# Queries and keys of sequences 2 to 7 as three rounded matmuls, and small rows in PSUM

## The chip, the cores and the metric

One core of a Trainium2 chip runs the kernel. Its engines work side by side, each through its own queue in order: TensorE (PE, with its weight loads PEld), VectorE (DVE), ScalarE (ACT), GpSimd (POOL) and SyncE (SP), which issues most transfers. The metric is the device time of one execution in microseconds (us), the median over several runs. The kernel before takes 412.45 us (three runs, 410.89 to 412.59).

## The reference

Eight sequences of 512 tokens with 128 features go through two layers, all in fp32. Each layer is an attention-like part times the silu of a mixture of experts (MoE), added to the input. The change is in layer 1:

```python
xn = _layernorm(x)                       # layer 1, its own layernorm
q = elu(xn @ Wq.T + bq) + 1              # feature maps
k = elu(xn @ Wk.T + bk) + 1
v = xn @ Wv.T + bv
out = linear_attention(q, k, v)          # causal, chunks of 128, running key_sum, kv_sum
s = out @ Wo.T + bo
scores = softmax(xn @ gate_w.T); top 2 of 8 experts per token
g = silu( sum over the top 2 of scores * ((silu(xe @ w1) * (xe @ w3)) @ w2)
          + (silu(xn @ w1s) * (xn @ w3s)) @ w2s )
x = x + s * g
```

## The kernel before

The program has three stretches. Up to some 55 us it normalises the input, routes the tokens of layer 0, and scatters them by group. Up to some 179 us it runs layer 0's experts on 35 sorted tiles, with layer 0's recurrences beside them. The rest is layer 1, one sequence `j` after the other, 0 to 7. The change lies in this last stretch.

Layer 1 is written out by hand as slots: every engine's queue runs `for j in range(8): for u in range(18)`, and its `if u == ...` lines say which piece stands in which slot. All experts are computed for all tokens: 8 experts and one shared unit, each with a gate half and an up half, give 18 slots.

- **PE** starts each slot with `gate_up(j, u)` (lines 948 to 966). To compute an fp32 product faster than fp32 matmuls do, the product is made of three fp32r ("rounded") matmuls into one PSUM bank: weights rounded times input rounded (L964), weights rounded times the input's rest (L965), weights' rest times input rounded (L966), where rest is value minus rounded value. In odd slots a `unit_down` (fp32, L986) follows. The attention pieces lie between: `scores` (L916) in slots 0 and 2, `sum_state` (L931), `turn_scores` (L910) in slot 5, `turn_result` (L991) in 7, `attend` (L943, L945) in 8.
- Sequence `k+1 = j+2` is prepared in the later slots of `j`: `turn_xn1` (four transposes, L891) in slot 13, `values` (L898) in 14, `query` (L903) in 15 and `key` (L906) in 16. `query` and `key` are plain fp32 matmuls of `a1w` with `xn1T`; the profile counts two matmuls for each.
- **DVE** empties each gate or up half with `scaled` (L1478: PSUM times the spread scores, to `gu`). `gate_up` of a slot waits until `scaled` of three slots earlier is done (`m_free`, a ring of three banks). Beside it: `variances` (L1356 to L1359) in slot 7, `ranks` and `scored` (L1388 to L1393) in 1 and 3, `gated` (L1343) and `added` (L1346) in 4 and 5.
- **ACT** applies silu (`unit_silu`, L658, table functions), copies `xn1T` out of PSUM (`xn1T_out`, L614) in slot 14 and rounds it (`round_of`, L619) in slot 5 of the next sequence, where it stands before `state_out` and `scoreT_out`.
- **POOL** multiplies the halves (`hidden1`, L443), makes `xc_rest` (`rest_of`, L430), the scales (L423, L425), `qT` and `kT` (`query_or_key`, L437), the result (L448) and the gathers of layer 0's output (L409).

The rounded input and its rest, `xc_round` and `xc_rest`, are kept in two buffer pairs, used in turn by even and odd sequences. `e1`, `pr` and `mv1` (the router's exponentials, its probabilities, the layernorm's means and variances) lie in SBUF: 128 partitions by 32, 32 and 8 values. A semaphore wait stands ahead of each instruction that needs another engine's result; `link` makes DVE wait for its own last result.

Of the kernel before, what the change touches and what calls it, by code (L numbers as in the profile page):

```python
# [6 lines left out]
ALU = mybir.AluOpType  # L7
# [47 lines left out]
REC_BANKS = (SEQS - LATE) * (6,) + LATE * (5,)  # L55
BANKS = (0, 1, 7)
CHUNK = TPS // 2
SCORE_BANKS = (6, 6, 4, 4)
# [25 lines left out]
def gated_recurrent_moe_two_layers(  # L84
# [4 lines left out]
    with ctx:  # L89
        def sb(name, shape, dt=F32):  # L90
            return ctx.enter_context(nc.sbuf_tensor(name, shape, dt))
# [24 lines left out]
        w0d = sb("w0d", [P, GROUPS * D0])  # L116
        a1w = sb("a1w", [P, 3 * P])
        a1b = sb("a1b", [P, 3])
        a1bn = sb("a1bn", [P, 2])
# [94 lines left out]
        def in_one_place(earlier, last):  # L214
# [25 lines left out]
        h0, h0T, gu = in_one_place(  # L240
            [[("h0", [P, 2, 512], F32), ("h0T", [P, 2, 512], F32)]], [("gu", [P, RING, 2, SEQ], F32)])

        HALF_E = E1 // 2 * SEQ
# [7 lines left out]
            w0_rounded w0_split f_turned f_xT f_xr f_gate f_up f_sg f_h f_hT f_hTs f_down f_y  # L251
            c_gy c_var c_rstd c_xn c_turned c_xT c_round c_rest w13_split c_q c_k c_relu c_expq c_qkT
            c_v c_lg c_lgm c_exp c_scores c_scoreT c_scoreT_out c_a c_at c_keys c_keys_out c_state c_state_out c_num c_s1
# [120 lines left out]
        def _(pool):  # L374
# [38 lines left out]
            def split_w13(p):  # L413
# [4 lines left out]
                                   ALU.subtract).then_inc(s["w13_split"], 1)  # L418

            def scales(k):  # L420
                pool.wait_ge(s["c_var"], k + 1)
                wait(pool, "c_xn", k)
                pool.tensor_tensor(rstd1[:, :], var1[:, :], minus_half[:, 0:TPS], ALU.pow).then_inc(s["c_rstd"], 1)  # L423
                pool.wait_ge(s["c_rstd"], 2 * k + 1)
                pool.tensor_tensor(nmr1[:, :], nmr1[:, :], rstd1[:, :], ALU.mult).then_inc(s["c_rstd"], 1)  # L425

            def rest_of(k):
                pool.wait_ge(s["c_round"], k + 1)
                wait(pool, "m_gu", SLOTS * (k - 1))
                pool.tensor_tensor(xc_rest[k % 2][:, :], xn1T[:, :], xc_round[k % 2][:, :].bitcast(F32),  # L430
                                   ALU.subtract).then_inc(s["c_rest"], 1)
# [22 lines left out]
            for p in range(PAIRS + 1):  # L454
                split_w13(p)
            gather(0)
            gather(1)
# [6 lines left out]
            for j in range(SEQS):  # L464
                hidden1(j, 1)
                if 0 < j < SEQS - 1:
                    query_or_key(j + 1, 1)
                hidden1(j, 2)
                if j + 1 < SEQS:
                    rest_of(j + 1)  # L470
                hidden1(j, 3)
                if j + 2 < SEQS:
                    scales(j + 2)
                if j == 0:
                    query_or_key(1, 1)
                hidden1(j, 4)
                if 0 < j < SEQS - 1:
                    query_or_key(j + 1, 0)
                if j > 0:
                    result1(j - 1)  # L480
                hidden1(j, 5)
                if j < PSEQ[1]:
                    gather(PSEQ[0] + j, slice(0, 2))
                if j == 0:
                    query_or_key(1, 0)
                hidden1(j, 6)
                if j < PSEQ[1]:
                    gather(PSEQ[0] + j, slice(2, 4))
                hidden1(j, 7)
                hidden1(j, 8)  # L490

        @block.scalar
        def _(act):
# [206 lines left out]
            for j in range(SEQS):  # L700
                k = j + 1
                for u in range(SLOTS):
                    if u == (0 if j < LAST else 1):
                        unit_silu(j, 0)
                    if u == 11 and k + 1 < SEQS:
                        normalised(k + 1)
# [8 lines left out]
                    if j == 0:  # L715
# [7 lines left out]
                        if u == 12:  # L723
                            scoreT_out(1, 4)
                    if u == 1 and 0 < j < SEQS - 1:
                        softmax_exp(k)
                        feature_exp(k)
                    if u == (1 if j == 0 else 5) and k < SEQS:
                        round_of(k)
                    if u == 1 and j == 0:  # L730
# [3 lines left out]
                    if k + 1 < SEQS:  # L734
                        if u == 3:
                            gy_silu(k + 1)
                        if u == 14:
                            xn1T_out(k + 1, 6)
                        if u == 16:
# [9 lines left out]
        def _(pe):  # L749
# [144 lines left out]
            def values(k, pair, bank):  # L894
# [4 lines left out]
                last.then_inc(s["c_v"], 1)  # L899

            def query(k, bank):
                pe.wait_ge(s["c_xT"], k + 1)
                pe.matmul(ps[:, bank, :], a1w[:, 0:P], xn1T[:, :], start=True, stop=True).then_inc(s["c_q"], 1)  # L903
# [45 lines left out]
            def gate_up(j, u):  # L949
                e, part = divmod(u, 2)  # L950
                n = SLOTS * j + u
                if u == 0:
                    pe.wait_ge(s["c_rest"], j + 1)
# [4 lines left out]
                par = j % 2  # L958
                last = n == SLOTS * SEQS - 1
# [90 lines left out]
            for j in range(SEQS):  # L1050
                k = j + 1
                for u in range(SLOTS):
# [62 lines left out]
        def _(dve):  # L1115
# [237 lines left out]
            def variances(k):  # L1353
                wait(dve, "c_xn", k)
                for t in range(TPS):
                    last = nc.vector.bn_aggr(mv1[:, t, :], st1[:, t, :])  # L1356
                link(last)
                nc.vector.tensor_scalar(nmr1[:, :], mv1[:, :, 0], -1.0, None, ALU.mult)
                nc.vector.tensor_scalar(var1[:, :], mv1[:, :, 1], LN_EPS, None, ALU.add).then_inc(s["c_var"], 1)  # L1359

            def values_out(k, pair, bank):
# [24 lines left out]
            def scored(k):  # L1386
                dve.wait_ge(s["c_exp"], k + 1)
                link(nc.vector.tensor_reduce(rs[:, :], e1[:, :, :], AX_X, ALU.add))  # L1388
# [4 lines left out]
                nc.vector.scalar_tensor_tensor(score[:, :, :].rearrange("p e t -> p t e"), rank[:, :, :], float(TOPK1),  # L1393
                                               pr[:, :, :], ALU.is_lt, ALU.mult).then_inc(s["c_scores"], 1)

# [92 lines left out]
            for j in range(SEQS):  # L1488
                k = j + 1
                for u in range(SLOTS):  # L1490
# [30 lines left out]
                    if k + 1 < SEQS:  # L1521
# [78 lines left out]
```

## Time and profile before

| | us |
|---|---|
| median of three runs | 412.45 |
| the profiled execution | 407.45 |
| its span, first to last instruction | 405.1 |
| PE busy in the span | 380.5 (94%) |
| DVE busy | 267.9 (66%) |
| ACT busy | 225.2 (56%) |
| POOL busy | 219.7 (54%) |
| mean granted TensorE clock | 0.975 of full |

Matmuls are pipelined: a record of 592 ns for half an fp32 product contains the time in which the next is already streaming. In the chain of work that ended last, where one piece begins when the one before lets go, the same product has 0.86 us for both halves. The sections below take the cost of PE work from the chain, and the cost on the other engines from the means of single instructions.

### The profile page before, as it was taken

The numbers are of one execution on the slowest core, as the hardware profiler recorded it, in microseconds if no ns is written. First come the engines' busy times: TensorE is split into PE (matmuls) and PEld (weight loads), VectorE is DVE, ScalarE is ACT, GpSimd is POOL, SyncE is SP. The second block draws the span as 40 slices with busy tenths as digits, with TensorE's granted clock in tenths as the row PEclk, the third lists the DMA queues.
The fourth block names the chain that finished last, engine by engine and source line by source line (L and its number), as shares of the span: only waits on it lengthen the run. The fifth ranks groups of instructions, "written<-read, shape, count | busy, mean of one in ns | idle before, by whom it ended". The sixth has DMA issues, their size and how long they took to land.

```text
span 405.1 us, 6272 instructions
## 1 busy us (share of the span) xinstructions
PE 380.5 (94%) x1874; PEld 285.3 (70%) x1874; DVE 267.9 (66%) x745; ACT 225.2 (56%) x447; POOL 219.7 (54%) x211
## 2 busy tenths in 40 slices
PE   7999877699997999899999999999999999999996
PEld 5684346588886888787667667677677677676784
DVE  5979943463342356528879769679689498677563
ACT  3685973355543565869664483574474664742321
POOL 4437887252007015106775857867949849267451
PEclk9868999899999899999999999999999999999999
DMA  8995311510031001036050150330510701503300
GB/s 229 270 359 230 107 39 52 151 38 2 0 104 47 9 2 28 0 124 209 24 214 0 43 220 0 117 145 2 212 51 0 262 1 29 207 0 98 139 26 26
DMA packets 26590, 38.63 MB, mean 95 GB/s; under 512 B 2496, under 2 KB 22848, under 8 KB 24128
## 3 DMA queue, kind: packets, MB, share of 16 engines
q1 hardware_dynamic: 24512, 34.03, 25.3%
q0 software_dynamic: 2048, 4.23, 3.4%
q8 instruction: 16, 0.26, 0.3%
q14 instruction: 14, 0.11, 0.1%
HBM read 29.20 MB, written 9.05 MB: 94 GB/s over the span
## 4 chain that ended last, share of the span: by engine, by line
PE 65%; DVE 11%; ACT 11%; issue 6%; another core or an unknown queue 4%; DMA 1%; POOL 1%; SPq 0%; DVEq 0%; ACTq 0%
PE ps L986 9%; PE ps L861 6%; PE ps L966 6%; PE ps L964 6%; PE ps L965 6%; PE ps L841 3%; PE ps L871 3%; PE ps L782 3%; PE ps L843 3%; PE ps L842 3%; PE ps L945 3%; PE ps L898 2%; PE ps L981 2%; DVE score L1393 2%
## 5 line engine op out<-in xcount | busy, mean ns | idle before, releaser
L443 POOL TENSOR_TENSOR gu<-gu 128x512 f32<-128x512 f32 x64 | 84.3, 1322 | 58.4 <-DVE gu L1478 53.5
L964 PE MATMUL ps<-xc_round,w_round 128*128 128x512 f32 (+1 forms) x145 | 82.2, 567 | 0.6 <-DVE gu L1456 0.6
L658 ACT ACTIVATE gu<-gu 128x512 f32<-128x512 f32 x64 | 40.4, 630 | 74.8 <-DVE gu L1478 74.7
L986 PE MATMUL ps<-gu,w2s 128*128 128x512 f32 x126 | 64.3, 592 | 0.0
L966 PE MATMUL ps<-xc_round,w_rest 128*128 128x512 f32 (+1 forms) x145 | 57.0, 393 | 0.0
L965 PE MATMUL ps<-xc_rest,w_round 128*128 128x512 f32 (+1 forms) x145 | 56.8, 392 | 0.0
L1478 DVE TENSOR_TENSOR gu<-ps,w_raw 128x512 f32<-128x512 f32 x64 | 43.7, 687 | 17.8 <-PE ps L966 14.9
L1319 DVE TENSOR_TENSOR sx_rest<-ps,sx_round 128x128 fp32r<-128x128 f32 x35 | 10.2, 292 | 64.4 <-ACT sx_round L571 58.5
L409 POOL DMA_INDIRECT xnT<-sorted_y,slot x32 | 31.3, 977 | 36.2 <-DMA sorted_y<-sorted_sb 28.4
L580 ACT COPY h0T<-ps 128x512 f32<-128x512 f32 x35 | 20.5, 587 | 52.2 <-PE ps L871 37.2
L861 PEld LDWEIGHTS ps<-w0d,h0T 128*128 128x128 f32 x280 | 37.7, 197 | 12.3 <-issue 9.5
L861 PE MATMUL ps<-w0d,h0T 128*128 x280 | 38.7, 283 | 8.2 <-ACT sorted_sb L585 7.2
L399 POOL DMA_INDIRECT sorted_rows<-sorted_sb,slot x32 | 37.2, 1161 | 14.8 <-issue 9.5
L841 PE MATMUL ps<-w_round,sx_round 128*128 x70 | 34.4, 492 | 5.2 <-DVE sx_rest L1319 3.8
L964 PEld LDWEIGHTS ps<-xc_round,w_round 128*128 128x128 f32 x145 | 27.5, 190 | 15.1 <-issue 11.4
L965 PEld LDWEIGHTS ps<-xc_rest,w_round 128*128 128x128 f32 x145 | 27.5, 190 | 13.7 <-issue 12.0
L1329 DVE SCALAR_TENSOR_TENSOR h<-sg,sorted_sb,ps 128x256 f32<-128x256 f32 x70 | 30.2, 473 | 4.0 <-PE ps L871 2.6
L966 PEld LDWEIGHTS ps<-xc_round,w_rest 128*128 128x128 f32 x145 | 27.2, 188 | 6.1
L1478 DVE TENSOR_TENSOR gu<-ps,w0d 128x512 f32<-128x512 f32 x32 | 21.7, 688 | 14.0 <-PE ps L966 13.9
L843 PE MATMUL ps<-w_rest,sx_round 128*128 x70 | 27.9, 399 | 0.0
L842 PE MATMUL ps<-w_round,sx_rest 128*128 x70 | 27.8, 398 | 0.0
L986 PEld LDWEIGHTS ps<-gu,w2s 128*128 128x128 f32 x126 | 23.6, 188 | 5.5 <-POOL gu L443 0.2
(203 smaller groups left out, 778.7 us busy)
## 6 DMA issues: line engine op xcount, KB each, us to landing
w_raw<-score_rows SPq DMA_DIRECT2D x8, 1024.0 KB
sorted_sb<-score_rows SPq DMA_DIRECT2D x4, 1024.0 KB
w0d<-score_rows SPq DMA_DIRECT2D x4, 1024.0 KB
sorted_rows<-zero_rows SPq DMA_DIRECT2D x1, 2340.0 KB, 15.6
xa<-in_x SPq DMA_DIRECT2D x8, 256.0 KB, 4.9
w_raw<-in_gate_up SPq DMA_DIRECT2D x1, 2048.0 KB
out_x<-xa SPq DMA_DIRECT2D x7, 256.0 KB
sorted_sb<-sorted_rows SPq DMA_DIRECT2D x1, 1690.0 KB, 7.9
```

The costliest lines, as they stand in the source:

```text
L399: pool.indirect_dma_start(sorted_rows, bass.IndirectOffsetOnAxis(ap=slot[:, t:t + 1], axis=0), rows[:, t, :], None).then_inc(scattered[h], 16)
L443: pool.tensor_tensor(gu[:, e % RING, 1, :], gu[:, e % RING, 0, :], gu[:, e % RING, 1, :], ALU.mult).then_inc(s["m_h"], 1)
L658: nc.scalar.activation(gu[:, e % RING, 0, :], gu[:, e % RING, 0, :], ACT.Silu).then_inc(s["m_sg"], 1)
L841: pe.matmul(bank, sx_round[:, par, :], w0_round[:, c], start=True, stop=False)
L842: pe.matmul(bank, sx_rest[:, par, :], w0_round[:, c], start=False, stop=False)
L843: return pe.matmul(bank, sx_round[:, par, :], w0_rest[:, c], start=False, stop=True)
L861: last = pe.matmul(ps[:, bank, 0:P], h0T[:, par, c * P:(c + 1) * P], w0d[:, bass.ds(g + c * P, P)], start=(c == 0), stop=(c == HC - 1))
L964: pe.matmul(bank, w13_round[:, c], xc_round[par][:, some], start=True, stop=False)
L965: pe.matmul(bank, w13_round[:, c], xc_rest[par][:, some], start=False, stop=False)
L966: pe.matmul(bank, w13_rest[:, c], xc_round[par][:, some], start=False, stop=True).then_inc(s["m_gu"], 1)
L986: pe.matmul(ps[:, 3, :], w2s[:, w * P:(w + 1) * P], gu[:, e % RING, 1, :], start=(e == 0), stop=(e == E1)).then_inc(s["m_y"], 1)
L1478: nc.vector.tensor_tensor(gu[:, p % RING, part, :], ps[:, BANKS[u % RING], :], spread[j % 2][(e - 1) // (E1 // 2)][:, c:c + SEQ], ALU.mult ...
```

## The change

For sequences 2 to 7 the query and key products are made of three fp32r matmuls (`in_three`), like the experts' products. POOL rounds the two weight matrices once and takes their rest (`split_qk`), after the same work for the experts' weights. Rounded input and rest must now be there before the queries, so they are made earlier: ACT rounds right behind `xn1T_out`, both now in slot 13, and DVE instead of POOL makes the rest, in slot 14, out of the PSUM bank that the transposes wrote. As the former sequences' buffers are still being read then, there is a third buffer pair, `xc2_round` and `xc2_rest`, in the place of an array that layer 0's weights used. PE's `turn_xn1` moves from slot 13 to slot 12, and ACT's `normalised` from slot 11 to 10 (which leaves its place in the queue as it was, since no silu stands between).

For the same sequences `e1`, `pr` and `mv1` lie in PSUM bank 6. ACT's softmax exponential writes there, so it now waits for DVE's first two masks of that bank (`c_at`), and stands behind the exponential of queries and keys instead of ahead of it.

```diff
+SMALL_BANK = 6
+        qk_round = sb("qk_round", [P, 2 * P], F32R)
+        qk_rest = sb("qk_rest", [P, 2 * P], F32R)
-        at, w0_round = in_one_place(
-            [[("at", [P, TPS, SEQ], F32)]], [("w0_round", [P, GROUPS * 2 * GU0], F32R)])
+        at, xc2_round, xc2_rest, w0_round = in_one_place(
+            [[("at", [P, TPS, SEQ], F32), ("xc2_round", [P, SEQ], F32R), ("xc2_rest", [P, SEQ], F32R)]],
+            [("w0_round", [P, GROUPS * 2 * GU0], F32R)])
-        xc_round, xc_rest = (xc0_round, xc1_round), (xc0_rest, xc1_rest)
+        xc_round, xc_rest = (xc0_round, xc1_round, xc2_round), (xc0_rest, xc1_rest, xc2_rest)
+        def small(first, n):
+            return ps[:, SMALL_BANK, first:first + n].rearrange("p (t c) -> p t c", t=TPS)
+        def e1_of(k):
+            return e1[:, :, :] if k < 2 else small(0, TPS * E1)
+        # pr_of(k), mv1_of(k): likewise
...
 POOL
+            def split_qk():
+                pool.wait_ge(s["attn1_in"], 16 * 4)
+                pool.tensor_copy(qk_round[:, :], a1w[:, 0:2 * P]).then_inc(s["qk_split"], 1)
+                pool.wait_ge(s["qk_split"], 1)
+                pool.tensor_tensor(qk_rest[:, :], a1w[:, 0:2 * P], qk_round[:, :].bitcast(F32),
+                                   ALU.subtract).then_inc(s["qk_split"], 1)
-                if j + 1 < SEQS:
-                    rest_of(j + 1)
+                if j == 0:
+                    rest_of(1)
...
 ACT
             def xn1T_out(k, bank):
-                wait(act, "c_rest", k)
+                if k in (1, 2):
+                    act.wait_ge(s["c_rest"], k)
             def round_of(k):
-                wait(act, "m_gu", SLOTS * (k - 1))
-                nc.scalar.copy(xc_round[k % 2][:, :], xn1T[:, :]).then_inc(s["c_round"], 1)
+                wait(act, "m_gu", SLOTS * (k - 2))
+                nc.scalar.copy(xc_round[k % 3][:, :], xn1T[:, :]).then_inc(s["c_round"], 1)
             def softmax_exp(k):
+                if k > 1:
+                    act.wait_ge(s["c_at"], TPS * (k - 1) + CHUNK)
-                nc.scalar.activation(e1[:, :, :], lg[:, :, :], ACT.Exp).then_inc(s["c_exp"], 1)
+                nc.scalar.activation(e1_of(k), lg[:, :, :], ACT.Exp).then_inc(s["c_exp"], 1)
...
 PE
+            def in_three(k, i, bank):
+                rest_ready(k)                    # waits c_rest_dve
+                pe.wait_ge(s["qk_split"], 2)
+                c, par = slice(i * P, (i + 1) * P), k % 3
+                pe.matmul(ps[:, bank, :], qk_round[:, c], xc_round[par][:, :], start=True, stop=False)
+                pe.matmul(ps[:, bank, :], qk_round[:, c], xc_rest[par][:, :], start=False, stop=False)
+                return pe.matmul(ps[:, bank, :], qk_rest[:, c], xc_round[par][:, :], start=False, stop=True)
-                        if u == 13:
+                        if u == 12:
                             turn_xn1(k + 1, 6)
-                            query(k + 1, 6)
+                            in_three(k + 1, 0, 6).then_inc(s["c_q"], 1)
-                            key(k + 1, 5)
+                            in_three(k + 1, 1, 5).then_inc(s["c_k"], 1)
...
 DVE
+            def rest_of(k, bank):
+                dve.wait_ge(s["c_round"], k + 1)
+                nc.vector.tensor_tensor(xc_rest[k % 3][:, :], ps[:, bank, :], xc_round[k % 3][:, :].bitcast(F32),
+                                        ALU.subtract).then_inc(s["c_rest_dve"], 1)
-                    last = nc.vector.bn_aggr(mv1[:, t, :], st1[:, t, :])
+                    last = nc.vector.bn_aggr(both[:, t, :], st1[:, t, :])     # both = mv1_of(k)
-                link(nc.vector.tensor_tensor(pr[:, :, :], e1[:, :, :], rs[:, :].unsqueeze(2).broadcast_to([P, TPS, E1]),
+                link(nc.vector.tensor_tensor(pr_of(k), e1_of(k), rs[:, :].unsqueeze(2).broadcast_to([P, TPS, E1]),
+                        if u == 14:
+                            rest_of(k + 1, 6)
```

How the queues stand in slots 12 to 16 of a middle sequence. PE before, from the last of `values` in slot 14 (L898) to the key in slot 16 (L906), with the query (L903) between:

```order
L898 MATMUL ps<-vg_w,xn1T 128x136 [waits c_xT,c_s1]
L898 MATMUL ps<-vg_w,xn1T 128x136
L964 MATMUL ps<-xc_round,w_round 128x512 [waits m_free]
L965 MATMUL ps<-xc_rest,w_round 128x512
L966 MATMUL ps<-xc_round,w_rest 128x512
L986 MATMUL ps<-gu,w2s 128x512 [waits m_h]
L903 MATMUL ps<-xn1T,a1w 128x512 [waits c_xT]
L964 MATMUL ps<-xc_round,w_round 128x512 [waits m_free]
L965 MATMUL ps<-xc_rest,w_round 128x512
L966 MATMUL ps<-xc_round,w_rest 128x512
L906 MATMUL ps<-xn1T,a1w 128x512
```

PE now, from slot 15's down product (L1027) on: L1005 to L1007 are the experts' three, L938 to L940 the new three.

```order
L1027 MATMUL ps<-gu,w2s 128x512 [waits m_h]
L938 MATMUL ps<-xc_round,qk_round 128x512 [waits qk_split,c_rest_dve]
L939 MATMUL ps<-xc_rest,qk_round 128x512
L940 MATMUL ps<-xc_round,qk_rest 128x512
L1005 MATMUL ps<-xc_round,w_round 128x512 [waits m_free]
L1006 MATMUL ps<-xc_rest,w_round 128x512
L1007 MATMUL ps<-xc_round,w_rest 128x512
L938 MATMUL ps<-xc_round,qk_round 128x512 [waits qk_split,c_rest_dve]
L939 MATMUL ps<-xc_rest,qk_round 128x512
L940 MATMUL ps<-xc_round,qk_rest 128x512
```

The query waits for DVE's rest where it waited for ACT's copy. DVE before, the `scaled` of slots 13 to 15 (L1478) and the first `values_out` (L1366, L1368):

```order
L1478 TENSOR_TENSOR gu<-ps,w_raw 128x512 [waits m_y,m_gu]
L1478 TENSOR_TENSOR gu<-ps,w_raw 128x512 [waits m_h,m_gu]
L1478 TENSOR_TENSOR gu<-ps,w_raw 128x512 [waits m_y,m_gu]
L1366 TENSOR_TENSOR vo<-ps,bv_wo 128x2x128 [waits c_exp,c_num,c_v]
L1368 COPY lg<-ps 128x16
```

DVE now, the same slots (L1525 is `scaled`, L1414 the new rest, L1408 and L1410 `values_out`):

```order
L1525 TENSOR_TENSOR gu<-ps,w_raw 128x512 [waits m_y,m_gu]
L1525 TENSOR_TENSOR gu<-ps,w_raw 128x512 [waits m_h,m_gu]
L1414 TENSOR_TENSOR xc_rest<-ps,xc_round 128x512 [waits c_round]
L1525 TENSOR_TENSOR gu<-ps,w_raw 128x512 [waits m_y,m_gu]
L1408 TENSOR_TENSOR vo<-ps,bv_wo 128x2x128 [waits c_exp,c_num,c_v]
L1410 COPY lg<-ps 128x16
```

The rest stands between two `scaled`, ahead of the one of slot 15. ACT before, and then now, from the silus of slots 11 and 13 (L658, now L684) on:

```order
L658 ACTIVATE gu<-gu 128x512 [waits m_free] x2
L614 COPY xn1T<-ps 128x512 [waits c_rest,c_k,c_turned]
L658 ACTIVATE gu<-gu 128x512 [waits m_free]
L624 ACTIVATE tv<-ps,a1b 128x512 [waits c_qkT,c_q]
L625 ACTIVATE tg<-ps,a1bn 128x512
```

```order
L684 ACTIVATE gu<-gu 128x512 [waits m_free] x2
L638 COPY xn1T<-ps 128x512 [waits c_k,c_turned]
L643 CAST xc_round<-xn1T 128x512 [waits m_gu,c_xT]
L684 ACTIVATE gu<-gu 128x512 [waits m_free]
L648 ACTIVATE tv<-ps,a1b 128x512 [waits c_qkT,c_q]
```

The copy keeps its place behind the silu of slot 13; the rounding is new behind it, and is gone from the next sequence's slot 5.

## Rows read from the trace of the kernel before

**Rows 1.** Windows: us, then each engine's busy time (instructions), PE clock, DMA share, GB/s.

```profile
235.20:263.50 28.30, 28.07 (x125) 19.70 (x124) 22.68 (x55) 16.08 (x29) 20.67 (x19) 1.00 0.26 95
```

**Rows 2.** Chain of waits, sequence 2: start us, us, what.

```profile
237.40 0.65 PE ps L916 x4
...
245.60 0.28 PE ps L910
245.88 0.23 PE ps L964
...
258.22 0.07 issue
258.29 1.16 PE ps L898 x8
...
261.00 0.86 PE ps L903 x2
261.86 0.23 PE ps L964
...
262.56 0.86 PE ps L906 x2
```

**Rows 3.** Chain of waits, sequences 0 and 7.

```profile
198.21 0.11 PE ps L910
...
375.01 0.65 PE ps L916 x4
...
383.04 0.23 PE ps L964
```

**Rows 4.** Timeline of sequence 2, DVE and POOL: start us, us, engine, line, operation.

```profile
242.73 0.17 DVE L1388 TENSOR_REDUCE rs<-e 128x4 f32<-128x32 f32 x1
242.96 1.29 POOL L443 TENSOR_TENSOR gu<-gu 128x512 f32<-128x512 f32 x1 [3.76 <-DVE gu L1478]
243.15 1.15 DVE L1390 TENSOR_TENSOR pr<-e,rs 128x32 f32<-128x32 f32 x1
244.21 1.26 POOL L437 TENSOR_TENSOR kT<-tv,tg 128x512 f32<-128x512 f32 x1
244.33 1.21 DVE L1393 SCALAR_TENSOR_TENSOR score<-rank,pr 128x32 f32<-128x32 f32 x1
...
246.04 0.68 DVE L1343 TENSOR_TENSOR gy<-gy,sT 128x512 f32<-128x512 f32 x1
...
250.42 1.28 POOL L443 TENSOR_TENSOR gu<-gu 128x512 f32<-128x512 f32 x1
250.59 1.13 DVE L1358 TENSOR_SCALAR nmr<-mv 128x4 f32<-128x4 f32 x1
```

**Rows 5.** Single lines of DVE: count, shortest/median/longest ns, first and last start.

```profile
L1390 DVE TENSOR_TENSOR pr<-e,rs x8: 193/1144/1154, 169.7 to 355.9; 128x32 f32<-128x32 f32 x8
L1393 DVE SCALAR_TENSOR_TENSOR score<-rank,pr x8: 215/1212/1218, 169.9 to 357.1; 128x32 f32<-128x32 f32 x8
L1358 DVE TENSOR_SCALAR nmr<-mv x8: 170/1126/1133, 145.5 to 335.2; 128x4 f32<-128x4 f32 x8
L1478 DVE TENSOR_TENSOR gu<-ps,w_raw x64: 675/691/693, 196.5 to 384.5; 128x512 f32<-128x512 f32 x64
```

**Rows 6.** Timeline of sequence 2, slots 12 to 14, DVE and ACT.

```profile
256.20 1.28 DVE L1478 TENSOR_TENSOR gu<-ps,w_raw 128x512 f32<-128x512 f32 x2
256.92 0.63 ACT L658 ACTIVATE gu<-gu 128x512 f32<-128x512 f32 x1 [1.50 <-DVE gu L1478]
257.56 0.59 ACT L614 COPY xn1T<-ps 128x512 f32<-128x512 f32 x1
258.26 0.69 DVE L1478 TENSOR_TENSOR gu<-ps,w_raw 128x512 f32<-128x512 f32 x1 [0.78 <-PE ps L966]
```

**Rows 7.** Groups by line: busy us, mean ns of one, idle before and releaser.

```profile
L430 POOL TENSOR_TENSOR xc_rest<-xn1T,xc_round 128x512 fp32r<-128x512 f32 x8 | 10.2, 1272 | 5.9 <-ACT xc_round L619 5.9
L634 ACT ACTIVATE tg<-tg 128x1024 f32<-128x1024 f32 x8 | 8.4, 1045 | 0.0
```

More of the change, by code:

```diff
@@ L241, in gated_recurrent_moe_two_layers, with pr_of, mv1_of @@
             [[("h0", [P, 2, 512], F32), ("h0T", [P, 2, 512], F32)]], [("gu", [P, RING, 2, SEQ], F32)])
+        def small(first, n):
+            return ps[:, SMALL_BANK, first:first + n].rearrange("p (t c) -> p t c", t=TPS)
+        def e1_of(k):
+            return e1[:, :, :] if k < 2 else small(0, TPS * E1)
+        def pr_of(k):
+            return pr[:, :, :] if k < 2 else small(TPS * E1, TPS * E1)
+        def mv1_of(k):
+            return mv1[:, :, :] if k < 2 else small(2 * TPS * E1, 2 * TPS)
         HALF_E = E1 // 2 * SEQ
@@ L251, in gated_recurrent_moe_two_layers @@
             w0_rounded w0_split f_turned f_xT f_xr f_gate f_up f_sg f_h f_hT f_hTs f_down f_y
-            c_gy c_var c_rstd c_xn c_turned c_xT c_round c_rest w13_split c_q c_k c_relu c_expq c_qkT
+            c_gy c_var c_rstd c_xn c_turned c_xT c_round c_rest c_rest_dve w13_split qk_split c_q c_k c_relu c_expq c_qkT
             c_v c_lg c_lgm c_exp c_scores c_scoreT c_scoreT_out c_a c_at c_keys c_keys_out c_state c_state_out c_num c_s1
@@ L428, in rest_of @@
                 pool.wait_ge(s["c_round"], k + 1)
-                wait(pool, "m_gu", SLOTS * (k - 1))
-                pool.tensor_tensor(xc_rest[k % 2][:, :], xn1T[:, :], xc_round[k % 2][:, :].bitcast(F32),
+                pool.tensor_tensor(xc_rest[k % 3][:, :], xn1T[:, :], xc_round[k % 3][:, :].bitcast(F32),
                                    ALU.subtract).then_inc(s["c_rest"], 1)
@@ L455, in _ @@
                 split_w13(p)
+            split_qk()
             gather(0)
@@ L704, in _ @@
                         unit_silu(j, 0)
-                    if u == 11 and k + 1 < SEQS:
+                    if u == 10 and k + 1 < SEQS:
                         normalised(k + 1)
@@ L725, in _ @@
                     if u == 1 and 0 < j < SEQS - 1:
+                        feature_exp(k)
                         softmax_exp(k)
-                        feature_exp(k)
-                    if u == (1 if j == 0 else 5) and k < SEQS:
-                        round_of(k)
+                    if u == 1 and j == 0:
+                        round_of(1)
                     if u == 1 and j == 0:
@@ L736, in _ @@
                             gy_silu(k + 1)
-                        if u == 14:
+                        if u == 13:
                             xn1T_out(k + 1, 6)
+                            round_of(k + 1)
                         if u == 16:
@@ L899, in values, with rest_ready @@
                 last.then_inc(s["c_v"], 1)
+            def rest_ready(k):
+                if k < 2:
+                    pe.wait_ge(s["c_rest"], k + 1)
+                else:
+                    pe.wait_ge(s["c_rest_dve"], k - 1)
+            def in_three(k, i, bank):
[5 more added lines that the diff above has]
+                return pe.matmul(ps[:, bank, :], qk_rest[:, c], xc_round[par][:, :], start=False, stop=True)
             def query(k, bank):
@@ L952, in gate_up @@
                 if u == 0:
-                    pe.wait_ge(s["c_rest"], j + 1)
+                    rest_ready(j)
                 e = unit_at(j, e)
@@ L957, in gate_up @@
                 wait(pe, "m_free", n - RING + 1)
-                par = j % 2
+                par = j % 3
                 last = n == SLOTS * SEQS - 1
@@ L1354, in variances @@
                 wait(dve, "c_xn", k)
+                both = mv1_of(k)
                 for t in range(TPS):
-                    last = nc.vector.bn_aggr(mv1[:, t, :], st1[:, t, :])
+                    last = nc.vector.bn_aggr(both[:, t, :], st1[:, t, :])
                 link(last)
-                nc.vector.tensor_scalar(nmr1[:, :], mv1[:, :, 0], -1.0, None, ALU.mult)
-                nc.vector.tensor_scalar(var1[:, :], mv1[:, :, 1], LN_EPS, None, ALU.add).then_inc(s["c_var"], 1)
+                nc.vector.tensor_scalar(nmr1[:, :], both[:, :, 0], -1.0, None, ALU.mult)
+                nc.vector.tensor_scalar(var1[:, :], both[:, :, 1], LN_EPS, None, ALU.add).then_inc(s["c_var"], 1)
             def values_out(k, pair, bank):
@@ L1387, in scored @@
                 dve.wait_ge(s["c_exp"], k + 1)
-                link(nc.vector.tensor_reduce(rs[:, :], e1[:, :, :], AX_X, ALU.add))
+                link(nc.vector.tensor_reduce(rs[:, :], e1_of(k), AX_X, ALU.add))
                 link(nc.vector.reciprocal(rs[:, :], rs[:, :]))
-                link(nc.vector.tensor_tensor(pr[:, :, :], e1[:, :, :], rs[:, :].unsqueeze(2).broadcast_to([P, TPS, E1]),
+                link(nc.vector.tensor_tensor(pr_of(k), e1_of(k), rs[:, :].unsqueeze(2).broadcast_to([P, TPS, E1]),
                                              ALU.mult))
@@ L1393, in scored @@
                 nc.vector.scalar_tensor_tensor(score[:, :, :].rearrange("p e t -> p t e"), rank[:, :, :], float(TOPK1),
-                                               pr[:, :, :], ALU.is_lt, ALU.mult).then_inc(s["c_scores"], 1)
+                                               pr_of(k), ALU.is_lt, ALU.mult).then_inc(s["c_scores"], 1)
             dve.wait_ge(sorted_in[0], 16)
```

## The prediction

> **What bounds the kernel now.** I read three views in this order: the windows by sequence, to see which engine is full in layer 1; the chain of waits through one sequence, to see where that engine is late; then the timeline around each such place, to see why. In the window of sequence 2, TensorE is busy for 28.07 of 28.30 us at a granted clock of 1.00, DVE for 22.68, POOL for 20.67, ACT for 16.08 [rows 1]. So layer 1 is bound by PE, and the reader should expect that work on another engine pays only where PE waits for it.
>
> The chain shows two such waits in each sequence. The first is at `turn_scores` (L910), which starts at 245.60, right behind DVE's score [rows 2, 4]. Its size comes from two equal stretches, from the first `scores` to the start of slot 6's product. In sequence 2 it is 245.88 - 237.40 = 8.48 us. In sequence 7 the same PE work is done without L910: 383.04 - 375.01 = 8.03 us. L910 takes 0.11 us where nobody is waited for [rows 3]. That leaves 8.48 - 8.03 - 0.11 = 0.34 us of waiting. As it is one sequence of six, read to a few hundredths, I take 0.3. The second wait is 0.07 us ahead of `values` (L898), for the copy `xn1T` [rows 2]: the copy ends at 257.56 + 0.59 = 258.15 and L898 starts at 258.29 [rows 2, 6].
>
> Why is the score late? The multiply for `pr`, 32 values per partition, takes 1.15 us, and the score 1.21 us. The shortest of the same lines are 0.19 and 0.22 us [rows 4, 5]. Each long one ends within 0.1 us of the end of a POOL instruction that had begun before it: 244.30 against 244.25, 245.54 against 245.47. The `nmr` of the variances does so too, 251.72 against 251.70 [rows 4]. All three have only SBUF operands. `scaled` (L1478), one operand in PSUM and one in SBUF, varies by 18 ns over 64 instructions, though POOL is busy most of the time [rows 1, 5]. So DVE stands still behind POOL in these three, and does not in instructions with an operand in PSUM.
>
> The Trainium skill ("SBUF — State Buffer", section "Who interferes with whom") has this as a rule: a DVE instruction with two SBUF inputs, or a 2-port mode one such as tensor_scalar, shares a port pair with GpSimd, and the second to start blocks wholly. The trace agrees for the three. The rule also speaks against the change: `gated` (L1343) has two SBUF inputs, and the change brings it forward into POOL's time. That is weighed below.
>
> **The change part by part.**
> *Queries and keys.* An fp32 product takes 0.86 us of the chain, 261.86 - 261.00. An expert's three take 262.56 - 261.86 = 0.70 us [rows 2]. The new three have the same shapes. Each replaced product gives back 0.16 us; with two for each of sequences 2 to 7, 12 x 0.16 = 1.9 us. That lies on the path, as PE is full. The three measured here begin right behind an fp32 product, which is where the query's will begin too (behind the down product of slot 15), so I take no extra.
>
> *Small rows in PSUM.* Of the three blocked instructions `pr` and the score lose up to 1.15 - 0.19 = 0.96 and 1.21 - 0.22 = 0.99 us, so the score comes 1.95 us earlier, against 0.3 us that PE waits. The wait goes in each of sequences 1 to 6: 6 x 0.3 = 1.8 us. Behind it L910 waits for nothing else. The exponential that feeds the score moves behind ACT's longer one, 1.04 us later [rows 7]. That one begins in slot 1, and DVE's first read of the result at 242.73 [rows 4] is in slot 3, two product slots and a down product later on PE (over 2 us), so I count 0 and would see a late exponential as an idle DVE ahead of its first sum. No row before shows DVE writing to PSUM. Bounds for `pr`: 0.19 us as if unblocked, 1.15 us as if still blocked. At either end the score alone, which has one SBUF input left, gives 0.99 us, three times the wait. `nmr` saves 0.95 us of DVE, off the path.
>
> *Turn one slot earlier.* The transposes cost PE the same in slot 12. Their data is ready without help: the transposes before came after a down product (0.86) and a gate product (0.70) more, and ACT's normalising stands at the same place in its queue. The copy to `values` now has 0.70 + 0.86 us more of cover, but stands behind the silu of slot 13, which starts only after `scaled` of slot 12. That silu runs 256.92 to 257.55 and the copy ends 258.15 [rows 6], so if DVE were as late as now, the 0.07 us would stay. DVE is less late by nearly the 0.95 us of `nmr`, so I count the 0.07 as gone: 6 x 0.07 = 0.4 us; its lower bound is 0.
>
> *Rounding and rest.* ACT's rounding, as wide as its copy (0.59 us), only changes place, and follows the copy by 0.6: done near 258.8 at the latest. DVE's rest is as wide as `scaled` and has its operand kinds, 0.69 us [rows 5]. It follows `scaled` of slot 14, which ends 258.26 + 0.69 = 258.95 [rows 6], so the rest is there at 259.6. The query stands at 261.00 [rows 2]: cover 1.4 us. Both sides move together when PE gains. Behind the rest on DVE wait `scaled` of slot 15 and `values_out`; slot 15's product ends on PE after 260.1, so they are not held. DVE's sum over a sequence: -0.96 - 0.99 - 0.95 + 0.69 = -2.2 us. POOL loses 1.27 us [rows 7], which stood ahead of its product for slot 7 and the scales; nothing on PE waits for these now, so I count 0.
>
> *Rounding the weights on POOL*, once, two instructions, is cheaper than one rest and rounding of the experts' 512 columns. It lies before the gathers, where POOL waits for layer 0's output; 0.
>
> Sum: 1.9 + 1.8 + 0.4 = 4.1 us. The profiled execution took 407.45 us (span 405.1), so it would take 403.3. The median of before is 5.0 us above that execution; nothing in layer 1's clock (1.00) explains it, and I take the difference to stay: 412.45 - 4.1 = 408.4 us, 1.0% faster.
>
> **The rivals.**
> *A. The rows in PSUM free nothing*, since the destination in PSUM or the remaining SBUF operand still keeps DVE behind POOL. Then PE goes on waiting 0.3 us, and only 1.9 to 2.3 us come: about 410.3. For it: no row shows such a write. Against it: the 18 ns of L1478 [rows 5].
>
> *B. Part of it is given back.* `gated` now follows a score that ends near 243.6, and `scaled` after it near 244.4, inside POOL's L437, which runs 244.21 to 245.47; before it stood at 246.04, free, 0.68 us [rows 4]. Blocked, it costs DVE up to 1.1 us, as `pr` and the score do now. `scaled` of slot 5 then ends near 246.8, and the PE product that needs its bank is slot 8's, near 248.1 after the gain (L910 at 245.3, then products of 0.70, 0.70, 0.86 and the turned result, by the chain's prices). So it is covered by more than 1 us. By the skill's rule the wait would merely move from two instructions that PE awaits to one that it doesn't; by the sum it costs 0. If two such blocks fall together, PE loses 0.2 to 0.5 us a sequence: 409.5 to 411.5.
>
> *C. Slower: the new preparation is late.* One mechanism: ACT's copy stands behind the silu of slot 13, that behind DVE's `scaled` of slot 12. Now they start at 256.20, 256.92 and 257.56, one right behind the other [rows 6], and the copy is just in time for PE. If a blocked time such as that of `pr` and the score together, 0.96 + 0.99 = 1.95 us, fell ahead of that `scaled`, the copy would come as much later, and PE would stand 1.9 us before `values`, six times: 408.4 + 11.4 = 419.8 us. It decides from 4.1 / 6 = 0.7 us of PE wait per sequence. Against it: DVE has 2.2 us less to do, and the block on `nmr`, which makes it late there, goes.
>
> **How the numbers follow.** Forecast 0.64, A 0.10, B 0.17, C 0.05; 0.04 for a gain above 6 us, if DVE's and POOL's lead also shortens stretches in sequences 0 and 7. The likeliest gives 408.4 us. The low end has half of those 4 us more: 406.4. The high end takes in A and most of B: 411.3. What a measurement tells from no change is about 0.5%, 2.1 us: faster means under 410.4. The forecast is nearly wholly there, A half, B a third: 0.78. Slower is C and a little: 0.06. The same: 0.16.
>
> **What would show it.** Right: one L910 without DVE ahead of it and 0.11 us in the chain; `pr` and the score near 0.2 us, `nmr` near 0.17 us; three 0.23 us pieces for query and key; 0.7 us less for each sequence than before; no DVE piece in the chain of sequences 1 to 6. Wrong: an idle PE ahead of `values` or of the first new part, which names ACT or DVE (C); `pr` still at 1.15 us (A); `gated` at 1.7 us with PE waiting for a bank in slot 8 (B). A clock below 1.00 in layer 1 would upset all of it.

## The result, and the profile after

| | before | after |
|---|---|---|
| median of four runs, us | 411.67 | 403.59 |
| lowest and highest | 408.44, 412.59 | 402.41, 403.96 |
| the profiled execution | 407.45 | 403.38 |
| its span | 405.1 | 400.5 |

The ratio is 0.9899, with a 95% interval of 0.9850 to 0.9948. All later runs were on three chips on which the kernel before took 400.4 to 400.6 us. There the changed kernel took 395.28 us against 400.63: 0.9860 (0.9823 to 0.9896). The kernel is faster, by 1.0 to 1.4%. One execution of a later kernel (`pr` in SBUF) took 626.42 us at a mean granted clock of 0.557; its ratio below leaves it out.

As the whole time differs between the first comparison and the later ones by more than the change is worth, all that follows is read from layer 1, where the granted clock is 1.00 (but for two stretches of the last experiment). The measure is the period of a sequence: the time from the first `attend` piece of one to that of the next in the chain of waits. Of the chain before (start us, us, what), the first and the last of six that bound the middle sequences:

```profile
221.01 0.67 PE ps L945 x6
...
362.00 0.67 PE ps L945 x6
```

After, the same two:

```profile
221.06 0.67 PE ps L986 x6
...
357.46 0.67 PE ps L986 x6
```

Five periods took 362.00 - 221.01 = 140.99 us, 28.20 each, and now 136.40 us, 27.28 each: 0.92 us less. Over six sequences that is 5.5 us. The span is only 4.6 us shorter, since layer 1 started about 1 us later in this execution. The microsecond was lost in layer 0: in both traces PE stood still for some 3.5 us until 132.5 us, and from 132 to 138 us the granted clock was then 0.50, where before it was 0.72; from 138 to 182 us it was 1.00 in both. The traces of the later runs have no such stand there, and their layer 1 starts some 8 us sooner (the first `attend` of the changed kernel at 187.30 us, here at 195.68). The periods don't depend on it: the later trace of the changed kernel has 27.29 us.

The window that answers to [rows 1], after:

```profile
235.20:263.50 28.30, 28.30 (x130) 20.66 (x129) 23.25 (x57) 17.24 (x31) 21.02 (x19) 1.00 0.32 115
```

PE is busy for all of it. The chain of waits of the same sequence, to be laid beside [rows 2]:

```profile
244.40 0.45 PE ps L972 x4
244.85 0.11 PE ps L951
...
257.07 0.24 PE ps L1007
257.30 0.93 PE ps L925 x8
...
258.92 0.86 PE ps L1027 x2
259.78 0.23 PE ps L938
260.01 0.24 PE ps L939
260.25 0.23 PE ps L940
```

No DVE, ACT or issue piece is left. `turn_scores` (L951) takes its bare 0.11 us. The query is three pieces of 0.23 to 0.24 us (L938 to L940). And `values` (L925) takes 0.93 us, where L898 took 1.16 behind a wait of 0.07 [rows 2]: the prediction had no step for that.

The single lines of DVE that answer to [rows 5] (count, shortest/median/longest ns, first and last start), and POOL's `kT`:

```profile
L1437 DVE TENSOR_TENSOR ps<-ps,rs x6: 198/200/200, 215.2 to 351.6; 128x32 f32<-128x32 f32 x6
L1440 DVE SCALAR_TENSOR_TENSOR score<-rank,ps x6: 208/211/215, 215.5 to 351.8; 128x32 f32<-128x32 f32 x6
L1400 DVE TENSOR_SCALAR nmr<-ps x6: 160/161/163, 194.9 to 330.3; 128x4 f32<-128x4 f32 x6
L1384 DVE TENSOR_TENSOR gy<-gy,sT x8: 680/682/702, 142.8 to 325.3; 128x512 f32<-128x512 f32 x8
L1387 DVE SCALAR_TENSOR_TENSOR xa<-gy,xa x8: 691/1050/1061, 143.5 to 326.7; 128x512 f32<-128x512 f32 x8
L459 POOL TENSOR_TENSOR kT<-tv,tg x8: 1272/1750/1767, 186.4 to 352.7; 128x512 f32<-128x512 f32 x8
```

`pr`, the score and `nmr` now take 0.20, 0.21 and 0.16 us in all six sequences. That POOL is busy beside them shows in the timeline of sequence 2, to be laid beside [rows 4]:

```profile
242.30 1.29 POOL L465 TENSOR_TENSOR gu<-gu 128x512 f32<-128x512 f32 x1 [3.32 <-DVE gu L1525]
...
242.51 0.20 DVE L1437 TENSOR_TENSOR ps<-ps,rs 128x32 f32<-128x32 f32 x1
...
242.74 0.21 DVE L1440 SCALAR_TENSOR_TENSOR score<-rank,ps 128x32 f32<-128x32 f32 x1
...
243.50 0.68 DVE L1384 TENSOR_TENSOR gy<-gy,sT 128x512 f32<-128x512 f32 x1
243.56 1.77 POOL L459 TENSOR_TENSOR kT<-tv,tg 128x512 f32<-128x512 f32 x1
...
244.83 1.05 DVE L1387 SCALAR_TENSOR_TENSOR xa<-gy,xa 128x512 f32<-128x512 f32 x1
```

`gated` (L1384) isn't blocked; POOL's `kT`, which starts inside it, is (1.75 us at the median, where the one of [rows 4] took 1.26), and so is `added` (L1387) behind it. Nobody on PE waits for either.

The preparation, in DVE's and ACT's timeline of the same sequence:

```profile
255.41 0.63 ACT L684 ACTIVATE gu<-gu 128x512 f32<-128x512 f32 x1 [1.60 <-DVE gu L1525]
255.95 0.57 ACT L638 COPY xn1T<-ps 128x512 f32<-128x512 f32 x1
256.55 0.62 ACT L643 CAST xc_round<-xn1T 128x512 fp32r<-128x512 f32 x1
257.95 0.68 DVE L1414 TENSOR_TENSOR xc_rest<-ps,xc_round 128x512 fp32r<-128x512 f32 x1
```

The copy ends at 256.52, 0.8 us ahead of `values`; the rest ends at 258.63, 1.15 us ahead of the query. The first weight load of `values`, shown next, begins at 256.91: from the copy to that it is 0.4 us.

Why is `values` shorter? PEld's timeline shows it. Here `xn1T` is the stationary operand, so the first weight load itself needs the copy. Before:

```profile
258.26 0.99 PEld L898 LDWEIGHTS ps<-vg_w,xn1T 128*128 128x128 f32 x8 [0.48 <-issue]
258.29 0.47 PE L898 MATMUL ps<-vg_w,xn1T 128*128 128x136 f32 x2
```

After:

```profile
256.91 1.12 PEld L925 LDWEIGHTS ps<-vg_w,xn1T 128*128 128x128 f32 x8
257.14 1.09 PE L925 MATMUL ps<-vg_w,xn1T 128*128 128x136 f32 x8
```

Now the first load is done while the gate product still streams, and the matmul follows 0.23 us behind the start of the load. Before, load and matmul began together, after the wait, and the load was paid for by PE. The same shows at `turn_scores`, whose stationary operand is the score. Before, its load began only when DVE's score was done, 0.01 us ahead of the transpose at 245.60 [rows 2]:

```profile
245.59 0.09 PEld L910 LDWEIGHTS ps<-cst,score 128*32 128x32 f32 x1 [0.36 <-DVE score L1393]
```

The piece took 0.28 us there and takes 0.11 now. Of the 0.3 us priced as a wait, 0.17 were this.

### The profile page after: what moved, and what is told of

The parts are those of the page before. It is cut to its first block, busy times and chain, and to the rows that moved or that the text cites. A ratio compares the mean times of both kernels' runs of the same rounds, so it can differ in the third digit from the quotient of the medians.

```text
span 400.5 us, 6309 instructions
## 1 busy us (share of the span) xinstructions
PE 375.9 (94%) x1886; PEld 289.1 (72%) x1886; DVE 262.2 (65%) x751; ACT 226.5 (57%) x447; POOL 215.3 (54%) x207
## 4 chain that ended last, share of the span: by engine, by line
PE 77%; ACT 11%; issue 4%; another core or an unknown queue 3%; DVE 2%; DMA 1%; SPq 1%; POOL 1%; ACTq 0%; DVEq 0%
PE ps L1027 13%; PE ps L1007 8%; PE ps L1005 8%; PE ps L1006 8%; PE ps L888 7%; PE ps L868 4%; PE ps L869 3%; PE ps L898 3%; PE ps L870 3%; PE ps L986 3%; PE ps L957 2%; PE ps L809 2%; PE ps L1022 2%; PE ps L925 2%
## 5 line engine op out<-in xcount | busy, mean ns | idle before, releaser
L465 POOL TENSOR_TENSOR gu<-gu 128x512 f32<-128x512 f32 x64 | 85.2, 1334 | 58.1 <-DVE gu L1525 54.6
L1005 PE MATMUL ps<-xc_round,w_round 128*128 128x512 f32 (+1 forms) x145 | 79.7, 549 | 0.6 <-DVE gu L1503 0.5
L684 ACT ACTIVATE gu<-gu 128x512 f32<-128x512 f32 x64 | 40.4, 631 | 65.2 <-DVE gu L1525 60.6
L1027 PE MATMUL ps<-gu,w2s 128*128 128x512 f32 x126 | 64.3, 592 | 0.0
L1007 PE MATMUL ps<-xc_round,w_rest 128*128 128x512 f32 (+1 forms) x145 | 57.1, 394 | 0.0
L1525 DVE TENSOR_TENSOR gu<-ps,w_raw 128x512 f32<-128x512 f32 x64 | 43.9, 688 | 19.6 <-PE ps L1007 16.8
L415 POOL DMA_INDIRECT sorted_rows<-sorted_sb,slot x32 | 36.1, 1129 | 14.8 <-issue 9.5
L868 PE MATMUL ps<-w_round,sx_round 128*128 x70 | 35.3, 504 | 3.8 <-DVE sx_rest L1360 3.8
L1005 PEld LDWEIGHTS ps<-xc_round,w_round 128*128 128x128 f32 x145 | 27.4, 189 | 14.0 <-issue 8.8
L1007 PEld LDWEIGHTS ps<-xc_round,w_rest 128*128 128x128 f32 x145 | 27.2, 187 | 6.0
L1525 DVE TENSOR_TENSOR gu<-ps,w0d 128x512 f32<-128x512 f32 x32 | 22.0, 687 | 14.0 <-PE ps L1007 14.0
L1027 PEld LDWEIGHTS ps<-gu,w2s 128*128 128x128 f32 x126 | 23.7, 188 | 5.4
```

Of the source, the lines that this page charges most:

```text
L415: pool.indirect_dma_start(sorted_rows, bass.IndirectOffsetOnAxis(ap=slot[:, t:t + 1], axis=0), rows[:, t, :], None).then_inc(scattered[h], 16)
L465: pool.tensor_tensor(gu[:, e % RING, 1, :], gu[:, e % RING, 0, :], gu[:, e % RING, 1, :], ALU.mult).then_inc(s["m_h"], 1)
L684: nc.scalar.activation(gu[:, e % RING, 0, :], gu[:, e % RING, 0, :], ACT.Silu).then_inc(s["m_sg"], 1)
L868: pe.matmul(bank, sx_round[:, par, :], w0_round[:, c], start=True, stop=False)
L1005: pe.matmul(bank, w13_round[:, c], xc_round[par][:, some], start=True, stop=False)
L1007: pe.matmul(bank, w13_rest[:, c], xc_round[par][:, some], start=False, stop=True).then_inc(s["m_gu"], 1)
```

## The experiments

One chip ran the changed kernel, the rows alone, both with fp32 queries, and the changed one with rows in SBUF; a second the turn in slot 13, `pr` and `mv1` in SBUF and the copy in slot 15; a third the other two. Kernels of one chip share the runs of the kernel before, whose period is read from its one trace, that of the first comparison. "Period" is the mean of the five; "`values`" is its piece in the chain. Ratios are to the kernel before, with the 95% interval.

| kernel | period us | `values` us | ratio |
|---|---|---|---|
| before | 28.20 | 1.16 + 0.07 wait | |
| turn in slot 12 alone | 28.13 | 1.09 | 0.9970 (0.9943 to 0.9997) |
| rows in PSUM alone | 27.93 | 1.17 + 0.07 wait | 0.9946 (0.9919 to 0.9973) |
| both, fp32 queries and keys | 27.64 | 0.93 | 0.9895 (0.9863 to 0.9927) |
| changed, rows in SBUF | 27.79 | 1.09 to 1.10, once 1.17 behind a wait | 0.9916 (0.9881 to 0.9950) |
| changed, turn in slot 13 | 27.58 | 1.17 + 0.07 wait | 0.9910 (0.9871 to 0.9948) |
| changed | 27.28 | 0.93 | 0.9860 (0.9823 to 0.9896) |
| changed, `pr` in SBUF | 27.28 | 0.93 | 0.9835 (0.9746 to 0.9925) |
| changed, `mv1` in SBUF | 27.28 | 0.93 | 0.9841 (0.9773 to 0.9909) |
| changed, only `e1` in PSUM | 27.29 | 0.93, once 1.00 | 0.9860 (0.9817 to 0.9903) |
| changed, copy in slot 15 | 30.17 | 1.17 + 2.0 wait, twice more at a lower clock | 1.0265 (1.0192 to 1.0338) |

**The changed kernel again**, beside its parts.

> The changed kernel once more, to have it in the same rounds as its parts. Its trace has 27.28 us per sequence against 28.2 before; six such gains are 5.5 us, 1.3 to 1.4% of the time. If the rest of the program is the same, the ratio is 0.986 to 0.987; the first run's 0.990 is then its low side.

The period is that of the first comparison to a hundredth of a microsecond. This ratio, unlike the first, leaves the forecast's 0.990 just outside its interval, on the side of a larger gain.

**Rows in PSUM alone.** The kernel before, with

```diff
+        def e1_of(k):
+            return e1[:, :, :] if k < 2 else small(0, TPS * E1)     # pr_of, mv1_of likewise
+                if k > 1:
+                    act.wait_ge(s["c_at"], TPS * (k - 1) + CHUNK)
-                        softmax_exp(k)
                         feature_exp(k)
+                        softmax_exp(k)
```

> Only the small rows go to PSUM (with the wait and the order of the exponentials that this needs); queries and keys stay fp32, the turn stays in slot 13. My theory: L910 no longer waits, 0.3 us per sequence, while the wait ahead of values stays, since the copy hangs on the turn in slot 13: 27.9 us per sequence, 1.8 us in all, ratio 0.995 to 0.996. Rival: DVE's lead of some 2.9 us also frees the values, then 27.6 us per sequence and 3.6 us in all.

The period fell by 0.27 us: this is the wait at `turn_scores`. But `values` still waited, though `nmr` was short. The chain, and ACT's copy in the timeline:

```profile
251.19 0.07 issue
251.26 1.17 PE ps L912 x8
```

```profile
250.53 0.59 ACT L626 COPY xn1T<-ps 128x512 f32<-128x512 f32 x1 [0.58 <-PE ps L905]
```

ACT stood idle for 0.58 us ahead of the copy, until the transposes (L905) were done. So it is PE's own transposes that make the copy late in slot 13, even when ACT is free. In the kernel before, the silu ends at 257.55 [rows 6] and the transposes, by the chain, at 257.52: two releasers within 0.03 us, of which I had named one.

**The turn alone.** The kernel before, with

```diff
-                        if u == 13:
+                        if u == 12:
                             turn_xn1(k + 1, 6)
```

> The kernel before with nothing but the turn in slot 12. In the run with three-part products and rows in SBUF, the copy hung on the silu of slot 13 and values took 1.10 us without a wait ahead. My theory: the same here, as DVE is as late as before: the 0.07 us go and values lose 0.07 of their 1.17, so 28.2 - 0.14 = 28.05 us per sequence, the wait at L910 stays. Rival: the turn alone frees the values, 0.93 us, 27.9 us per sequence.

The wait ahead of `values` goes, but only just: with DVE as late as before, the copy stands behind the silu again. Chain, and PEld:

```profile
249.28 0.23 PE ps L966
249.51 1.09 PE ps L898 x8
```

```profile
249.40 0.76 PEld L898 LDWEIGHTS ps<-vg_w,xn1T 128*128 128x128 f32 x6 [0.33 <-issue]
```

The copy ends at 249.29, the first load begins at 249.40, too late to hide, and `values` takes 1.09 us. PE didn't stand still ahead of it here, and still it cost 0.16 us more than 0.93; so it isn't the stand as such that makes `values` dear, as one of the expectations below has it, but the late load. The kernel lost 1.23 - 1.09 = 0.14 us there, yet four of its periods are 28.11 to 28.12 us, 0.08 less than before's, and the fifth is 28.20. Where the rest went back is open.

**Both, with fp32 queries and keys.** The kernel of the rows alone, with the turn in slot 12.

> Rows in PSUM and the turn in slot 12, queries and keys in fp32 with two buffer pairs. My theory: both waits go, values take 0.93 us instead of 1.16, as an engine that has stood still needs some 0.2 us more for its next group: 28.2 - 0.3 - 0.3 = 27.6 us per sequence; the changed kernel's 27.28 is then 0.32 less, 2 x 0.16. Rival: the 0.23 us of values have nothing to do with the wait but with the three-part neighbours; then values stay at 1.16 us and the sequence at 27.8.

```profile
248.82 0.23 PE ps L980
249.05 0.93 PE ps L912 x8
```

0.93 us needs both edits: the turn frees the copy from the transposes, the rows free it from a late silu. Against the rows alone the turn is worth 0.30 us a sequence (27.93 to 27.64, before rounding 27.932 to 27.636), where alone it was worth 0.07. And from here to the changed kernel is 27.64 - 27.28 = 0.36 us, the price of two products: 0.18 each. In the chain the two new products take 0.70 and 0.69 us in place of 0.86 each; the last 0.03 us of the 0.36 lie in hundredths of their neighbours.

**The changed kernel with the rows in SBUF.**

```diff
         def e1_of(k):
-            return e1[:, :, :] if k < 2 else small(0, TPS * E1)
+            return e1[:, :, :]                                      # pr_of, mv1_of likewise
```

> The changed kernel with the small rows left in SBUF: the three-part queries and keys, the third buffer pair, the turn in slot 12. My theory: the 0.3 us at L910 stays, the products give 12 x 0.16 = 1.9 us; the values' wait depends on whether DVE is late at the scaled of slot 12. If it goes: 28.2 - 0.32 - 0.3 = 27.6 us per sequence; if it stays: 27.9. Rival: without the rows in PSUM DVE gets the rest on top of its blocked time and PE waits ahead of the first new part, over 28.2 us per sequence, slower than before.

The blocks are back, with `turn_scores` at 0.28 us behind them, and `values` starts just in time, at 1.10 us:

```profile
L1437 DVE TENSOR_TENSOR pr<-e,rs x8: 193/1143/1149, 161.2 to 344.7; 128x32 f32<-128x32 f32 x8
L1440 DVE SCALAR_TENSOR_TENSOR score<-rank,pr x8: 215/1212/1216, 161.5 to 345.9; 128x32 f32<-128x32 f32 x8
```

```profile
248.34 0.24 PE ps L1007
248.58 1.10 PE ps L925 x8
```

Four of its periods are 27.71 to 27.74 us; one is 28.04, with a real wait ahead of `values`. Without the rows the preparation stands at the edge.

**The changed kernel with the turn in slot 13.**

```diff
-                        if u == 12:
+                        if u == 13:
                             turn_xn1(k + 1, 6)
```

> The changed kernel with the turn back in slot 13; ACT's copy and rounding and DVE's rest stay where they are. My theory: the copy then hangs on the turn, PE waits 0.07 us ahead of values and these take 1.17 us: 27.28 + 0.30 = 27.6 us per sequence, +1.8 us in all. The rest still comes over 1 us ahead of the query. Rival: the rest comes too late as well, PE waits ahead of the first new part, and the sequence takes over 28 us.

0.30 us a sequence came back, 0.07 as a wait and 0.24 in `values`. The rest was still there for the query: the earlier turn isn't needed for the three parts.

**`pr`, then `mv1`, back in SBUF; then both.** Three kernels, each the changed one with

```diff
         def pr_of(k):                                               # or mv1_of, or both
-            return pr[:, :, :] if k < 2 else small(TPS * E1, TPS * E1)
+            return pr[:, :, :]
```

> The changed kernel with pr in SBUF, e1 and mv1 in PSUM. pr then has one SBUF input, the score two. My theory: pr takes 0.2 us, the score is blocked by POOL for about 1 us, and since it alone is late PE does not wait at L910: 27.28 us per sequence. Rival: what blocks is the SBUF destination; then pr takes over 1 us too, and L910 waits as before, 27.6 us.

> The changed kernel with mv1 in SBUF, e1 and pr in PSUM. My theory: nmr is blocked again or not, by where POOL stands; even at 1.1 us DVE has caught up by slot 12, since pr and the score no longer delay it: 27.28 us per sequence, values 0.93. Rival: it was nmr's place right ahead of slots 8 to 12 that made the copy late; then values wait again, 27.5 to 27.6 us.

> The changed kernel with only e1 in PSUM, pr and mv1 in SBUF. With pr alone in SBUF the score took 0.94 us, with mv1 alone nmr took 1.11 us, each at no cost to PE. My theory: both together still cost PE nothing, 27.28 us per sequence, since the score at 0.94 us ends ahead of L910 and DVE has caught up by slot 12: e1 alone carries the gain of the rows. Rival: the two blocks add up as in the kernel before, the copy comes late and values take 1.1 us or more: 27.45 to 27.6 us.

The single lines with `pr` in SBUF:

```profile
L1437 DVE TENSOR_TENSOR pr<-ps,rs x6: 191/191/192, 207.3 to 343.7; 128x32 f32<-128x32 f32 x6
L1440 DVE SCALAR_TENSOR_TENSOR score<-rank,pr x8: 219/938/942, 163.0 to 343.9; 128x32 f32<-128x32 f32 x8
L1384 DVE TENSOR_TENSOR gy<-gy,sT x8: 684/1208/1216, 134.9 to 318.1; 128x512 f32<-128x512 f32 x8
```

The multiply reads `e1` from PSUM and isn't blocked, wherever it writes; in sequence 2 it starts 0.20 us behind the start of a POOL product of 1.29 us. The score, now with both inputs in SBUF, is (0.94 us), and so is `gated`, which meets a POOL instruction in the new place (1.21 us). `nmr` with `mv1` in SBUF is blocked again (1.11 us at the median). No mean period moved by more than 0.01 us: one of the two blocks, of 0.96 and 0.99 us, was enough to take away, and `mv1` is off the path. `e1` alone in PSUM gives nearly all of it. But two of its six `values` took more, the first 1.11 us (ahead of the five periods) and the fourth 1.00, so with it alone the preparation stands nearer the edge.

**ACT's copy and rounding in slot 15 for the middle sequences**, to price a late copy, as in rival C.

```diff
-                        if u == 13:
+                        if u == (15 if j > 0 else 13):
                             xn1T_out(k + 1, 6)
                             round_of(k + 1)
```

> The changed kernel with ACT's copy and rounding behind the silu of slot 15 in sequences 1 to 5 (rival C of the prediction, put in on purpose). scaled of slot 14 ends some 0.73 us after values begin now; silu and copy add 1.25 us. My theory: PE stands 2.1 us ahead of values and these take 0.23 us more: 29.6 us per sequence in five sequences, 11 to 12 us slower than the changed kernel, some 6 us slower than before. Rival: the queue behind PE takes the wait up later in the sequence and less than 1 us per sequence is lost.

The chain of sequence 2:

```profile
251.04 0.25 PE ps L1007
...
251.31 0.70 DVE gu L1525
...
252.57 0.58 ACT xn1T L638
...
253.28 1.17 PE ps L925 x8
```

PE stands 253.28 - 251.29 = 2.0 us. Three of the five periods are 29.5 us: 2.25 us more, which is the wait and the 0.24 of `values`. The other two are 31.1 us, with the same wait. The windows of a stretch behind it, in one of the three and then in one of the two (columns as in [rows 1]):

```profile
257.00:262.00 5.00, 5.00 (x23) 3.68 (x21) 2.83 (x9) 4.42 (x7) 2.42 (x2) 1.00 0.44 177
282.80:288.00 5.20, 5.19 (x18) 3.94 (x19) 1.80 (x4) 0.62 (x2) 4.67 (x5) 0.67 1.03 386
```

and that one's chain:

```profile
282.67 0.14 issue
282.81 1.64 PE ps L925 x8
284.45 0.43 PE ps L1005
```

The granted clock fell from 2.4 GHz to 1.2 right behind the 2.0 us in which PE stood: 0.43 us a matmul in place of 0.23, until 287.16 us, where they take 0.23 again. That is 1.6 us more in each of the two sequences.

## Why the prediction was right, and where it was off

The ratio was forecast at 0.990 and measured at 0.9899, then 0.9860; the profiled execution was forecast at 403.3 us and took 403.38. Both look better than they are. The median, 403.59 us, lies 4.8 us under the forecast and under the low end of its range, 406.4. The profiled execution came out by luck, by two errors that cancel: layer 1 gave 5.5 us where the sum had 4.1, and layer 0 took back about 1 us (with 0.5 us more outside the span). The absolute forecast of 408.4 us rested on before's median of 412.45, 5.0 us above its profiled execution; in the comparison before had 411.67 and after stood only 0.2 us above its own. That level isn't the change's, and with one profile of each kernel nothing here tells what sets it.

Step by step, for six sequences:

| step | forecast us | measured us | by |
|---|---|---|---|
| 12 products | 12 x 0.16 = 1.9 | 6 x 0.356 = 2.1 | both edits against the changed kernel |
| wait at `turn_scores` | 6 x 0.3 = 1.8 | 6 x 0.266 = 1.6 | rows alone |
| wait ahead of `values` | 6 x 0.07 = 0.4 | 6 x 0.296 = 1.8 | rows alone against both |
| sum | 4.1 | 5.5, as by the periods | |

The split of the last two rows goes by the order in which the edits are made. Rows first give 0.27 and then the turn 0.30 us a sequence; the turn first gives 0.07 and then the rows 0.49.

*The mis-sized term* is the third: 0.4 us in the sum, 1.8 us measured. I priced the wait as the 0.07 us in which the chain shows nobody at work. A wait ahead of PE costs more than its gap where the awaited data is the stationary operand: the first weight load then can't run beside the matmul before. That was 1.16 - 0.93 = 0.23 us on top, and it stood in the trace before, in PEld's rows, which I hadn't read. The wait at `turn_scores` has the same hidden part, 0.17 us, and was priced nearly right (0.3 against 0.27), since its price came from two whole stretches and not from the gap. Also its cause was half right. I held the copy to be late behind the silu alone, and counted on `nmr`. The rows alone, which shorten `nmr`, left the wait whole; the transposes held the copy as well, and it took both edits.

*Small rows in PSUM.* Right: unblocked at 0.20 us, the lower of the two bounds. Rival A is refuted: neither the destination in PSUM nor the one SBUF input left keeps DVE behind POOL, whose product runs from 242.30 to 243.59 over both. That one block less would be enough was the prediction's argument, and `pr` in SBUF shows it.

*Rival B.* Its mechanism is real, its place moved. `gated` comes at 243.50 and isn't blocked, but holds POOL's `kT`, and `added` is blocked behind it (1.05 us). With `pr` in SBUF `gated` itself is blocked, at 1.21 us. In neither does PE wait. The rule of the Trainium skill weighed in the prediction ("SBUF — State Buffer", section "Who interferes with whom"), that the second to start stands still, fits both: POOL's `kT` at 1.75 us behind DVE, and DVE's at 1.05 to 1.21 us behind POOL.

*Rival C.* It didn't come. The block that it feared never fell ahead of that `scaled`; the last experiment made the copy late by its place in ACT's queue. So it doesn't test the 1.9 us, but it shows what a late copy costs beyond the stand: PE stood 2.0 us each time, and with the dearer `values` and the clock the five sequences lost 150.9 - 136.4 = 14.5 us, where 5 x 2.0 = 10 would have been counted by the prediction's way. The changed kernel stays clear by 0.8 us ahead of `values` (0.4 us ahead of its first load) and 1.15 us ahead of the query (forecast 1.4).

*Rest and rounding* took 0.68 and 0.62 us, as forecast from `scaled` and the copy, and held nobody.

## What to carry to other kernels

Where PE waits for its stationary operand, price the wait as the gap plus the load that can no longer be hidden, here 0.07 + 0.23 us; an operand that comes just in time still costs 0.16. Look at both releasers of a late instruction: if two end within hundredths of each other, removing one is worth little until the other goes too (here the turn alone gave 0.07 us a sequence, and behind the rows 0.30). And of several blocks ahead of one wait, only as many need to go as exceed the wait: one array of three in PSUM gave the gain to 0.01 us a sequence.

## What the runs showed of the hardware beyond that

- DVE wrote 128x32 values to PSUM, with one input in PSUM and one in SBUF, in 0.20 us, and in 0.19 us to SBUF, both beside a busy POOL. With both inputs in SBUF the score took 0.94 to 1.21 us beside it, and `pr` 1.14.
- A DVE instruction of 0.68 us with two SBUF inputs lengthened the POOL instruction that started inside it from 1.27 to 1.75 us.
- `values`, eight matmuls of 136 columns, took 0.93 us with the first load ahead, 1.09 just in time, and 1.17 behind a wait.
- A stand of PE of 2.0 us was followed by a clock of 0.67 to 0.72 over the next 5 to 6 us in two cases of five; behind the other three it stayed at 1.00. What tells them apart is open. A stand of some 3.5 us in layer 0 was followed by 0.72 over 132 to 138 us in the trace of before and by 0.50 in that of after.
